# A four-layer graph network: the resident blocks of the adjacency products are loaded from GpSimd's queue, the streamed pieces from SyncE's

## What is computed

```
# layer 0, three times:  x = segment_sum(x[row] * norm[:, None], col)
# layer 1, once:         neigh_sum = segment_sum(feat[src] * weight[:, None], dst)
# layer 2, twice:        Tx = segment_sum(w[:, None] * x[src], dst)
# layer 3, attention over the same edges:
att = expAtt / (segment_sum(expAtt, rows)[rows] + 1e-08)
out = segment_sum(att[:, :, None] * v, rows)
```

## Time and profile before

| | |
|---|---|
| median of 3 runs | 2697.01 us (2692.9 to 2699.05) |
| the profiled execution | 2693.88 us, its span 2692.1 us |
| mean granted TensorE clock | 0.977 of full speed |
| busy, share of the span | DVE 69%, PE 46%, POOL 47%, ACT 29% |
| bytes read / written in HBM | 368.64 MB / 168.31 MB |

### The profile page before, as it was taken

The page is one execution under the profiler, slowest core; times in us unless marked ns, Lnnn a source line. Parts: engine busy times, 40 slices in busy tenths (PEclk is TensorE's granted clock), DMA queues, the critical chain, the costliest instruction groups (busy, mean ns, idle before and its releaser), DMA issues. The chain is left out here.

```text
span 2692.1 us, 40080 instructions
## 1 busy us (share of the span) xinstructions
PE 1234.0 (46%) x12303; PEld 596.1 (22%) x12303; DVE 1845.2 (69%) x3894; ACT 775.9 (29%) x1905; POOL 1266.3 (47%) x973
## 2 busy tenths in 40 slices
PE   1111111111111111111111079999999639898997
PEld 1111111111111111111111023334444313333334
DVE  9988888888888888888887110022211539999996
ACT  0000000133223332112031300000001149999996
POOL 2788888888888888888888300000000000101001
PEclk9999999999999999999999999999999769999997
DMA  7777777588888889777575899879867272333321
GB/s 226 238 210 207 224 197 224 127 201 218 214 206 217 218 203 224 162 161 168 110 166 114 219 395 424 321 316 414 351 233 314 76 127 86 88 88 88 87 86 45
DMA packets 487296, 537.82 MB, mean 200 GB/s; under 512 B 130048, under 2 KB 443709, under 8 KB 469053
## 3 DMA queue, kind: packets, MB, share of 16 engines
q1 hardware_dynamic: 124717, 290.41, 30.1%
q10 hardware_dynamic: 249904, 245.78, 28.3%
q0 software_dynamic: 112608, 0.85, 10.1%
HBM read 368.64 MB, written 168.31 MB: 199 GB/s over the span
## 5 line engine op out<-in xcount | busy, mean ns | idle before, releaser
L620 POOL DMA_INDIRECT table<-amount,cell x782 | 1210.6, 1548 | 295.5 <-issue 279.9
L441 DVE SCALAR_TENSOR_TENSOR equal<-key_row,keys,masks 128x1280 bf16<-128x1280 f32 (+9 forms) x790 | 692.2, 944 | 0.2 <-DVE parts L427 0.2
L573 PE MATMUL totals<-parts_g,equal 128*128 128x6 bf16 x4345 | 128.7, 167 | 1023.2 <-DVE is_tile L450 1023.2
L291 ACT ACTIVATE w_tile<-cells 128x128 f32<-128x128 f32 x600 | 179.2, 300 | 779.5 <-issue 769.0
L573 PEld LDWEIGHTS totals<-parts_g,equal 128*128 128x128 bf16 x4345 | 122.0, 104 | 1034.6 <-DVE is_tile L450 1034.6
L952 PE MATMUL banks<-ring,xs 128*64 128x512 f32 x1200 | 301.7, 605 | 7.5 <-DMA ring<-counts_dram 7.5
L1219 POOL COPY v_tile<-v_all 128x128 f32 x175 | 51.2, 294 | 505.6 <-PE banks_d L1272 431.9
L1209 POOL MEMSET o_t<- 128x64 f32 x1 | 0.2, 151 | 604.6 <-POOLq L727 604.6
L433 DVE SCALAR_TENSOR_TENSOR equal_tail<-key_row,keys,masks 128x1280 bf16<-128x1280 f32 x156 | 235.2, 1546 | 20.7 <-issue 17.6
L1257 PE MATMUL banks_d<-q,k 96*128 (+2 forms) x700 | 193.1, 367 | 80.6 <-DMA k<-parts_dram 47.4
L1104 ACT ACTIVATE att<-banks_d,shift 128x1024 f32<-128x1024 f32 (+1 forms) x175 | 199.5, 1140 | 75.3 <-PE banks_d L1257 75.0
(11 more groups left out here) (228 smaller groups left out, 1520.7 us busy)
## 6 DMA issues: line engine op xcount, KB each, us to landing
table<-zeros ACTq DMA_DIRECT2D x100, 800.0 KB, 6.4
cells<-table ACTq DMA_DIRECT2D x24, 3200.0 KB, 12.2
ring<-counts_dram SPq DMA_DIRECT2D x60, 1280.0 KB, 11.2
ring<-weights_dram SPq DMA_DIRECT2D x60, 1280.0 KB, 8.3
key_row<-keys_dram SPq DMA_DIRECT2D x79, 640.0 KB
weights_dram<-w_tile ACTq DMA_DIRECT2D x24, 1600.0 KB
counts_dram<-c_tile ACTq DMA_DIRECT2D x24, 1600.0 KB
count<-counts_dram SPq DMA_DIRECT2D x150, 256.0 KB, 2.9
```

Of the source, the lines that this page charges most:

```text
L291: ins = nc.scalar.activation(w_tile[:, b, s], cells[:, s, :, 0], ACT.Copy, accum_out=deg_parts[:, s, bass.ds(t, 1)])
L441: ins = nc.vector.scalar_tensor_tensor(equal[b][:, OWN_AT[j]:OWN_AT[j + 1]], key_row[:, b, j * P:GE], keys[:, bass.ds(g * G + j, 1)], own_ ...
L573: nc.tensor.matmul(sums, equal[b][:, at:at + P], parts_g[:, b, j, :], start=False, stop=True, skip_group_check=True)
L620: nc.gpsimd.indirect_dma_start(out=table, out_offset=bass.IndirectOffsetOnAxis(ap=cell[:, b, j:j + 1], axis=0), in_=amount[:, b, j, :], in ...
```

## The change

SyncE's program keeps the streamed pieces alone. The kept blocks and block 6 are issued by GpSimd, in the same order among themselves, with the same buffers, the same sizes and the same semaphores. For the counts GpSimd waits for nothing, so its eleven loads are issued from the start of the stage. For the weights it waits for `sums_ready` of the same block in propagation 2, as SyncE did, but no longer stands behind the streamed pieces in program order.

```diff
         @block.sync
         def _(sp):
             for prop in range(6):
-                dram, again = (counts_dram, prop > 0) if prop < 3 else (weights_dram, prop > 3)
+                dram = counts_dram if prop < 3 else weights_dram
                 for n in range(NC):
                     chunk = by_chunk(dram, n)
                     if n in STREAMED:
...
-                    elif not again:
-                        if prop:
-                            sp.wait_ge(sums_ready, NC * (prop - 1) + n + 1)
-                        if n in KEPT:
-                            r = KEPT.index(n)
-                            for q in range(PIECES):
-                                ss = slice(q * PIECE, (q + 1) * PIECE)
-                                sp.dma_start(resident[:, r, ss], chunk[:, ss]).then_inc(kept_landed[r][q], 16)
-                        else:
-                            sp.dma_start(last[:], chunk).then_inc(last_landed, 16)
+
+        @block.gpsimd
+        def _(pool):
+            for matrix, dram in enumerate((counts_dram, weights_dram)):
+                for n in range(NC):
+                    if n in STREAMED:
+                        continue
+                    chunk = by_chunk(dram, n)
+                    if matrix:
+                        pool.wait_ge(sums_ready, NC * 2 + n + 1)
+                    if n in KEPT:
+                        r = KEPT.index(n)
+                        for q in range(PIECES):
+                            ss = slice(q * PIECE, (q + 1) * PIECE)
+                            pool.dma_start(resident[:, r, ss], chunk[:, ss]).then_inc(kept_landed[r][q], 16)
+                    else:
+                        pool.dma_start(last[:], chunk).then_inc(last_landed, 16)
```

## The result

| | before | after |
|---|---|---|
| median | 2694.95 us (4 runs, 2690.86 to 2699.05) | 2736.07 us (4 runs, 2734.37 to 2743.04) |
| profiled execution, its span | 2693.88 us, 2692.1 us | 2734.81 us, 2733.1 us |

The changed kernel is 1.6% slower: ratio 1.0157, 95% interval 1.0132 to 1.0182, 41 us. Forecast were +29 us, 2726, in a range of 2705 to 2740.

The account below looks back on a forecast made before the run. Loads set the pace in propagation 0 alone, with 9.4 us of PE idle for loads. Steps of 10 + 11 + 8 = 29 us made 2693.9 into 2723 us profiled, median 2726 us; range 2705 to 2740.

Parts of the forecast that it names:

- rival A: Wherever both queues are full, each gets half of the bandwidth; 2718 to 2734 us; chance 0.70.
- rival C: In starved stretches (0.0, 0.2 with 0.3, 2.3, 3.0) the clock falls: up to +12 us; chance 0.11, shared with SP under half.
- Step 1: Propagation 0: GpSimd's early counts loads share bandwidth with streamed pieces wanted at once; block 1.0 ends late, +10 us.
- Step 2: Propagation 2, block 2.3: its streamed pieces share bandwidth with the weights that block 3.1 wants 70 us later; +11 us.
- step 3: Block 3.0: its pieces share bandwidth with loads for blocks 3.4 and 3.6, released by 2.4 and 2.6; +8 us.
- Nothing else: Rest of the kernel: no further cost; GpSimd's third stage begins behind the same barrier, its loads over 200 us earlier.
- rival B: Where the queues share, GpSimd's gets clearly less than half of the bandwidth; 2705 to 2714 us; chance 0.13.
- D: Where loads are the limit, the pair's higher rate makes good the mixing; 2697 us, at best 2688; chance 0.03.

Follow-up runs that it names:

- counts_only: Against the kernel before: GpSimd loads only the kept blocks of the counts, SyncE those of the weights in their old place; 2713.27 us.
- weights_only: Against the kernel before: GpSimd loads only the kept blocks of the weights, SyncE those of the counts in their old place; 2724.84 us.
- act_queue: Against the kernel before: kept blocks issued on ScalarE's queue, counts at the stage's start, weights behind the sums' copies in propagation 2; 2732.92 us (ratio 1.0136).
- interleaved_on_sp: Against the kernel before: SyncE issues everything, but the counts' kept loads go between the first eleven streamed pieces of propagation 0; 2704.99 us (ratio 1.0041).

## Why the prediction was right, and where it was off

**Direction, cause and places were right.** The share of one half is measured (695 to 697 packets), the rate of 6.18 us a piece is 6.17, and the three places where the time is lost are the three steps, 0.0 to 0.4, 2.3 and 3.0, with nothing in 1.1 to 2.2. Counts_only and weights_only lay each step at the door of its own loads. Two figures of what the profile after would show were off: PE waits 23.5 us on `ring` in propagation 0 and not 25 or 30, and block 4.0 begins at 1965.0 and not near 1952, 7.3 us of it from the first stage.

**The number was right with help.** The sum was 29 us and 41 were measured: 7.3 us come from a stage that the prediction put at nothing, and 4.4 from the products. 2736.07 lies above the 2734 at which rival A ended, and inside the range only because that left room for rival C, another cause.

**Step 1** was 10 and is 11.2 us (11.6 in counts_only, 11.3 in act_queue and interleaved_on_sp). Block 0.0 ended 15.4 us late where 14.8 were forecast, but two errors cancel in that: the fifth piece was in use 2.0 us earlier than forecast (30.8 us after the first clear, not 32.8) and took PE 5.3 us instead of 2.7. What counts is the end of 0.3, since PE waits for loads again in 0.2 and 0.3: 19.3 us late instead of 17. The last piece of 0.3 was in use 84.4 us after the first clear, 2.1 later than in the sum. The weight loads of PE show that it came that late, and was waited for:

```profile
1647.22 0.20 PEld L959 LDWEIGHTS banks<-ring,xs 128*64 128x64 f32 x3 [0.23 <-DMA ring<-counts_dram]
```

The sum let GpSimd's queue run empty one shared piece too early: the pieces at 1631.51 and 1637.95 still came 6.44 us apart, those behind them 3.09. In 0.4 to 1.0 PE then got back 8.1 us (forecast 7). The clock has no part in the 11.2: in interleaved_on_sp it was 1.00 in block 0.3 (1626 to 1642 us), and its last piece was waited for too and in use 84.5 us after the first clear:

```profile
1639.58 2.79 PE L963 MATMUL banks<-ring,xs 128*64 128x512 f32 x10 [0.30 <-DMA ring<-counts_dram]
```

**Steps 2 and 3** were 11 and 8 and are 12.7 and 11.1 us. Step 2 is again the loads: the fifth piece of 2.3 was forecast in use 20.9 us after the block's clear and came at 22.7:

```profile
1820.87 0.20 PEld L959 LDWEIGHTS banks<-ring,xs 128*64 128x64 f32 x4 [0.96 <-DMA ring<-counts_dram]
```

The ten matmuls of 5.38 us at 1811.82 (granted clock 0.50) are in the same block, but PE waited 0.80 us behind them, so they cost nothing, and the clock was 1.00 from 1818.0 on. Weights_only says the same: its last two pieces of 2.3 took 2.79 us each, and the step is 12.3. In step 3 the clock does cost something. The fifth piece landed 21.9 us after the clear of 3.0 (forecast 20.5), at 1875.44 by the trace's landing events, and PE was not there yet, for the ten matmuls ahead of it ran at 0.50:

```profile
1870.49 5.38 PE L959 MATMUL banks<-ring,xs 128*64 128x512 f32 x10 [3.77 <-DMA ring<-weights_dram]
...
1876.83 2.79 PE L959 MATMUL banks<-ring,xs 128*64 128x512 f32 x10
```

In weights_only the piece landed after 22.0 us, PE took it at once, and step 3 is 9.8 and not 11.1: 1.3 us for the clock, 1.4 for the later load. So rival C, held at up to +12 us, came to 1.3; the mechanism was as described there, slow matmuls in front of a wait are free. Why the loads came 1.4 to 2.1 us later than in the sum, beyond the piece named under step 1, is open.

**The 1.6 us won back in 3.6 to 4.1** are the clock, and chance. The earlier trace rows showed a wait of 2.50 us and ten matmuls of 5.14 us behind it. The changed kernel waits as long there, 2.51 us, and the ten take 3.98 us:

```profile
1963.64 0.43 PE L916 MATMUL banks<-w_self,h_t 65*128 65x64 f32 x2 [2.51 <-ACT h_t L776]
...
1965.52 3.98 PE L959 MATMUL banks<-ring,xs 128*64 128x512 f32 x10
```

The cost of this wait changes from one execution to the next: before_again, the same program as before, waits 2.50 us, its ten matmuls take 2.79 us, and it is 3.2 us shorter in 3.6 to 4.1. So every stage above that is compared with the profile of before can be up to 3 us off for this reason alone; the steps are not, for they lie ahead of it.

**The step that failed** is "*Nothing else*". It looked at what the change does behind the barrier and took the first stage as untouched, since no instruction of it moved. GpSimd's program had 782 scatters in it, each of which paid 12 ns for the presence of a plain load, 7.3 us in this profile. No row of before showed it. With it the forecast would have been 2733.

**The rivals.** B (GpSimd's queue gets less) and D (the pair moves more) are refuted by the queue rows: 50.6% to 50.4%, 425 GB/s. The stalled descriptors that rival B took from the Trainium skill, "SBUF — State Buffer", section "Who interferes with whom", did not come: ten loads are issued in 5.34 us, with VectorE busy for 4.70 us of the window from 1562.9 to 1568.3. The reading of the Trainium skill, "DMA: Bandwidth & Descriptors", section "Issuing engines are not separate DMA queues", as "the queue does not matter" was wrong by 33 us; the section's own words, that the loads interleave, are what the traces show (695 packets to 697), and interleaved_on_sp shows that in step 1 the interleaving is the whole cost. My estimate that a load takes GpSimd 1.9 us to issue was over three times too high, with no effect.

**Open.** Why a plain load in GpSimd's program lengthens its indirect DMAs by 12 ns is not known; whether a plain load ahead of the scatters does the same was not tried. Nor was a handing over of block 6 that costs nothing, or the weights' loads in the wrong order on one queue.

## What to carry to other kernels

When loads are the limit, the queue's order is the schedule: a second queue added no bandwidth here, it took every other packet, and what was issued early on it was paid for by what was wanted at once. Read the DMA share by stretch before moving loads; where it is 1.0, a prefetch with a deadline 70 us away belongs behind the loads with a deadline of 3 us, and if two queues must be used, let them hand over by semaphores, and look at each moment of release: a load of 1600 KB released too late or too early cost 3 to 8 us here. Compare the stages that an edit does not touch as well: here a fifth of the loss was there.

## What the hardware showed that was not expected

- GpSimd's indirect DMAs took 1546 ns in all five profiles of programs without a plain DMA on GpSimd, and 1558 or 1559 ns in all eight with one or more, down to one of 2 KB issued after the last of them.
- Two full queues, hardware with hardware (888 to 880) and software with hardware (695 to 697), had equal numbers of packets, also when the packets were of 4 KB and 10 KB (567 to 570, small ones counted): the queue with the larger packets got 2.8 times the bytes.
- The same wait of PE at the same place, 2.50 us, was followed by ten matmuls of 5.14 us in one execution and of 2.79 us in another of the same program; the stretch differed by 3.2 us.
- A plain load of 1280 KB takes GpSimd about 0.53 us to issue (ten in 5.34 us), about as long as SyncE (five in 2.61 us):

```profile
1562.89 5.34 POOL L759 DMA_DIRECT2D resident<-counts_dram  x10 [45.19 <-POOLq L196]
...
1562.34 2.61 SPq L744 DMA_DIRECT2D ring<-counts_dram  x5
```
